# Three attentions of a decoder kernel rebuilt: fp32 scores of four heads in one burst of eight

## What is computed

```python
q = (query @ Wq.T + bq) * SCALING          # query = layernorm(x), key = value = ctx
k = key @ Wk.T + bk
v = value @ Wv.T + bv
scores = jnp.einsum('bhld,bhsd->bhls', q, k) + attn_mask[None, None, :, :]
scores = jnp.where(key_padding_mask[:, None, None, :], -jnp.inf, scores)
probs = jax.nn.softmax(scores.astype(jnp.float32), axis=-1)
attn = jnp.einsum('bhls,bshd->bhld', probs, v)
return attn.transpose(0, 2, 1, 3).reshape(query.shape[0], query.shape[1], E) @ Wo.T + bo
# x = x + jnp.tanh(g_xattn[2]) * that
```

## Time and profile before

| | |
|---|---|
| median of 3 executions | 862.42 us |
| lowest, highest | 861.39, 3578.52 us |
| the profiled execution: its own time | 862.37 us |
| its span | 860.4 us, 14382 instructions |
| its mean granted TensorE clock | 0.898 of 2.4 GHz |
| PE busy, and its weight loads | 702.3 us (82%), 396.0 us (46%) |
| DVE, ACT, POOL busy | 573.1 us (67%), 488.9 us (57%), 166.6 us (19%) |

### The profile page before, as it was taken

How to read it: one execution, slowest core, us unless ns; L and a number is a source line. 1 busy time by engine, 2 the same in 40 slices (tenths; PEclk the granted TensorE clock), 3 DMA queues, 4 the chain that set the end, 5 groups by cost and what they waited for, 6 DMA issues and landing times. The chain is left out here.

```text
span 860.4 us, 14382 instructions
## 1 busy us (share of the span) xinstructions
PE 702.3 (82%) x4728; PEld 396.0 (46%) x4728; DVE 573.1 (67%) x1765; ACT 488.9 (57%) x1323; POOL 166.6 (19%) x135
## 2 busy tenths in 40 slices
PE   4589994559997878999744899949999999869978
PEld 2266663336665323333222667635336666644322
DVE  3699995869996358667865999855316666436553
ACT  2288881259883568598812988812666556413201
POOL 8622000420000045536655000020000000000000
PEclk8689997769999768998885999979999999969999
DMA  8895004060000000000009200000000000000000
GB/s 310 169 319 177 2 7 69 23 126 2 2 2 2 0 1 0 1 0 1 1 0 180 41 2 2 2 26 0 1 0 1 1 2 2 1 1 1 0 1 24
DMA packets 22056, 32.26 MB, mean 38 GB/s; under 512 B 1760, under 2 KB 15712, under 8 KB 21216
## 3 DMA queue, kind: packets, MB, share of 16 engines
q1 hardware_dynamic: 21984, 31.36, 14.4%
HBM read 21.39 MB, written 9.96 MB: 36 GB/s over the span
## 5 line engine op out<-in xcount | busy, mean ns | idle before, releaser
L816 ACT ACTIVATE RING<-RING,NMX 128x256 f32<-128x256 f32 x384 | 190.7, 500 | 56.2 <-DVE NMX L1637 55.8
L1637 DVE CUSTOM_DVE_ANT_0 RING<-bank,ADJM 128x256 f32<-128x256 f32 x384 | 143.4, 413 | 23.5 <-DMA scratch<-RING 22.5
L1158 PE MATMUL bank<-W,RING 128*128 128x128 f32 x768 | 120.5, 282 | 15.6 <-ACT RING L828 13.9
L541 POOL TENSOR_TENSOR small<-small 128x8 f32<-128x8 f32 (+2 forms) x13 | 17.7, 1365 | 463.1 <-DVE small L1528 463.1
L1158 PEld LDWEIGHTS bank<-W,RING 128*128 128x128 f32 x768 | 91.7, 145 | 27.9 <-ACT RING L816 23.2
L1138 PE MATMUL bank<-ARENA 128*128 128x256 bf16 x384 | 77.8, 290 | 30.7 <-DMA ARENA<-scratch 25.7
L1649 DVE COPY RING<-bank 128x512 f32<-128x512 f32 x144 | 98.6, 686 | 1.2 <-PE bank L1158 0.8
L816 ACT ACTIVATION_READ_ACCUMULATOR RING<-RING,NMX 128x1 f32 x384 | 72.8, 190 | 0.0
L997 PE MATMUL bank<-XT,W 128*128 128x512 f32 (+2 forms) x118 | 62.2, 668 | 6.6 <-ACT XT L712 5.3
L728 ACT ACTIVATE RING<-bank,NMX 128x512 f32<-128x512 f32 x64 | 43.4, 683 | 41.8 <-PE bank L1062 21.2
L1280 PE MATMUL bank<-ARENA,W 64*128 64x512 f32 x180 | 62.3, 710 | 3.6 <-DVE ARENA L1830 2.3
(11 more groups left out here) (253 smaller groups left out, 1307.3 us busy)
## 6 DMA issues: line engine op xcount, KB each, us to landing
scratch<-ARENA SPq DMA_DIRECT2D x18, 256.0 KB, 3.2
ARENA<-scratch SPq DMA_DIRECT2D x6, 768.0 KB, 10.6
W<-in_weights SPq DMA_DIRECT2D x1, 2564.0 KB, 21.2
scratch<-RING SPq DMA_DIRECT2D x36, 64.0 KB, 3.0
ARENA<-scratch SPq DMA_DIRECT2D x12, 192.0 KB, 3.8
scratch<-RING SPq DMA_DIRECT2D x18, 128.0 KB, 2.9
ARENA<-scratch SPq DMA_DIRECT2D x6, 384.0 KB, 6.6
W<-in_weights SPq DMA_DIRECT2D x2, 1024.0 KB, 13.7
```

The lines of the kernel that those rows point to most:

```text
L816: nc.scalar.activation(P_OF(n)[:, q * S:(q + 1) * S], S_OF(n)[:, q, :], ACT.Exp, bias=NMX[:, 2 * t + q:2 * t + q + 1], scale=-1.0, accum_o ...
L1158: mm = nc.tensor.transpose(bk[:, o:o + P], P_OF(n)[:, i:i + P], ident)
L1637: nc.vector.tensor_tensor_reduce(out=S_OF(n)[:, q, :], in0=SBANK(n)[:, q * S:(q + 1) * S], in1=ADJM[:, b, q, :], scale=-1.0, scalar=BIG, o ...
```

## The change

- Scores are fp32 on the 8 rows of a head. Keys and queries are made with each head at the start of a 32-partition strip (`heads`: four narrow matmuls, 32 columns of the array each, into one bank), so that four heads lie in the four strips. The bf16 parts, the DRAM scratch and its DMAs, and the clearing of QS and KS go.
- A unit becomes one query tile of two heads. Every four units PE issues the eight score matmuls of four heads and two query tiles in one run, heads j = 0 to 3 into banks 0 to 3, and `Scores.fill` makes it wait for all eight DVE reductions of the run before. There is no second set of score banks.
- V has a column of ones behind each head's 8 columns (`PITCH` = 9), so that P times V gives the row sums too: the exponential loses `accum_out`. The result is transposed back (`ONE_T`), DVE takes a reciprocal and multiplies 64 elements, and once a sequence the packed result is transposed again (`BACK_T`) and multiplied by compact output weights WOC (one matmul and one row in place of four and one for each tile).
- DVE and ACT each copy every second unit's transposes.
- For attentions 0 and 2 only the keys of sequences 0 and 1 and the queries of sequence 0 are made ahead of the loop. Values, keys of sequences 2 and 3, and the queries of 1 and of 2 and 3 are made inside it (`extra`, at t = 4, 16, 8 and 24), in the score banks, between two runs of scores. Attention 1 has its keys and values made beside layer 0's linear layer, and only the two later pieces of queries are extras.
- In attention 0 only sequence 0's masks are made ahead of the loop; the rest (`other_masks`) is done by DVE at t = 6, POOL adding to it; POOL makes half of the later attentions' masks earlier.

The diff, cut to its core:

```diff
-LAG, PV_T, OTR_T, SEL_T, OUT_T = 3, 8, 9, 13, 27
-PT_SLOTS = 7
+LAG, PV_T, OTR_T, ONE_T, BACK_T, OUT_T, END_T = 3, 8, 9, 13, 27, 31, 16
...
+EXTRAS = [[("q", 0), ("v", 0), ("q", 1), ("k", 2), ("q", 2)], [("q", 0), ("q", 1), ("q", 2)],
+          [("q", 0), ("v", 0), ("q", 1), ("k", 2), ("q", 2)]]
...
# PE
+            def heads(out, name, g, rhs):
+                for j in range(HG):
+                    f = DH * (HG * g + j)
+                    mm = nc.tensor.matmul(out[PAD * j:PAD * j + PAD, :], w(name, f, f + PAD), rhs, start=True,
+                                          stop=True)
+                return mm
...
+            def extra(a, kind, k, scores):
+                x, (t0, t1) = extra_no(a, kind, k), PIECES[k]
+                scores.fill(pe, [(s_xa, 2 * x + 2), (s_xd, 2 * x + 2)])
+                for g in range(NG):
+                    if kind == "q":
+                        mm = heads(bank[g][:, 0:t1 - t0], f"wq{a}", g, XT[:, t0:t1])
...
-                        for q in range(2):
-                            mm = nc.tensor.matmul(bk[:, q * S:(q + 1) * S],
-                                                  QS[:, h, b * S + q * P:b * S + (q + 1) * P],
-                                                  KS[:, h // 2, b * S:(b + 1) * S], start=True, stop=True)
-                        mm.then_inc(s_s, 1)
+                        scores.fill(pe, [(s_max, 2 * base + 4 * m + 8)])
+                        for q in range(TPB):
+                            for j in range(HG):
+                                r = slice(PAD * j, PAD * j + DH)
+                                mm = nc.tensor.matmul(bank[j][:, q * S:(q + 1) * S],
+                                                      QT[r, g, b * S + q * P:b * S + (q + 1) * P],
+                                                      KT[r, g, b * S:(b + 1) * S], start=True, stop=True)
+                                if j % 2 == 1:
+                                    mm.then_inc(s_s, 1)
...
+                    if t >= ONE_T and (t - ONE_T) % 4 == 0 and (t - ONE_T) // 4 < UNITS // 4:
+                        for q in range(TPB):
+                            mm = nc.tensor.transpose(bank[7][:, q * P:(q + 1) * P],
+                                                     OTR[:, GG % 2, q * P:(q + 1) * P], ident)
+                        mm.then_inc(s_one, 1)
...
# ACT
                             nc.scalar.activation(P_OF(n)[:, i * S:(i + 1) * S], S_OF(n)[:, i, :], ACT.Exp,
-                                                 accum_out=SUMS[:, 2 * t + q:2 * t + q + 1]
...
# DVE
+                        if a != 1 and t == 4:
+                            dve.wait_ge(s_zero, 1 if a < 2 else 2)
+                            extra(a, "v", 0)
+                        if a == 0 and t == 6:
+                            other_masks()
+                        if a != 1 and t == 16:
+                            extra(a, "k", 2)
+                        if t in (8, 24):
+                            extra(a, "q", t // 16 + 1)
-                        dve.wait_ge(s_s, n + 1)
+                        dve.wait_ge(s_s, base + t // 4 * 4 + 3 + jj)
...
-                    if 0 <= u < UNITS and u % 4 != 2:
+                    if 0 <= u < UNITS and u % 2 == 0:
...
+                        dve.wait_ge(s_one, GG + 1)
+                        link(nc.vector.reciprocal(RS, src[:, :, :, DH:PITCH]))
+                        nc.vector.tensor_tensor(
+                            ON[:, i % 2, :, PAD * g:PAD * g + PAD].rearrange("p q (j d) -> p q j d", j=HG),
+                            src[:, :, :, 0:DH], RS.to_broadcast([P, TPB, HG, DH]), ALU.mult).then_inc(s_on, 1)
```

More of the change, by code:

```diff
@@ L515, in _ @@
-            read_keys(2)
-            queries(2)
+            compact(2)
             sp.wait_ge(s_var, 9)
@@ L545, in roots, with masks @@
                 root(TPB, NT)
-            def masks(a):
+            def masks(a, b0, b1):
                 if a > 0:
                     pool.wait_ge(s_max, 2 * UNITS * a)
-                for b in range(B):
+                for b in range(b0, b1):
                     for q in range(TPB):
@@ L1013, in turn, with biases @@
                     n_xn[0] += 1
-            def keys(a):
-                for c in range(NC):
-                    product(rk, [(w(f"wk{a}"), CT[:, half(c)])], s_fk)
+            def biases():
+                at = COL["cols"][0] + CI["bk0"][0]
+                for h in range(H16):
+                    g, j = h // HG, h % HG
+                    mm = nc.tensor.matmul(bank[5][PAD * j:PAD * j + PAD, 6 * g:6 * g + 6],
+                                          w("ident", DH * h, DH * h + PAD), W[:, at:at + 6], start=True, stop=True)
+                mm.then_inc(s_bk, 1)
@@ new lines, in heads, with keys, value_tiles @@
+            def heads(out, name, g, rhs):
[4 more added lines that the diff above has]
+                return mm
+            def keys(a, c):
+                for g in range(NG):
+                    heads(rh.fill(pe)[:, :], f"wk{a}", g, CT[:, half(c)]).then_inc(s_hf, 1)
+            def value_tiles(a, out, t0, t1):
+                for t in range(t0, t1):
+                    mm = nc.tensor.matmul(out[:, (t - t0) * D:(t - t0 + 1) * D], CT[:, t * P:(t + 1) * P],
+                                          w(f"wv{a}"), start=True, stop=True)
+                return mm
@@ new lines, in attention @@
+                            pe.wait_ge(s_to, 2 * GG + 2)
+                            pe.wait_ge(s_otr, GG)
+                            if G == 0:
+                                pe.wait_ge(s_ea, ra.n)
+                                if a != 1:
+                                    extra_done(a, "v", 0)
+                        for j in range(HG):
+                            f = PITCH * (HG * g + j)
+                            mm = nc.tensor.matmul(bank[6][PAD * j:PAD * j + PAD, 0:S], V[:, 2 * b + part, f:f + PAD],
+                                                  PT[:, GG % 2, j, part, :], start=(part == 0), stop=(part == 1))
```

578 lines of the change are left out of this document (279 added, 299 removed).

## The result

| | before | changed |
|---|---|---|
| median | 862.59 us (4 executions; the 862.42 ahead is of three) | 882.84 us (4 executions, 874.03 to 884.88) |
| ratio to before | 1 | 1.022, 95% interval 1.0133 to 1.0306 |
| profiled execution, its span | 862.37, 860.4 us | 882.24, 880.1 us |
| mean granted TensorE clock | 0.898 | 0.917 |

The kernel became slower by 20 us; whether by more than 2% the interval leaves open. The forecast was 856.5, with 880 as the upper end of its range. The page's first part, for the changed kernel: busy us, share of the span, instructions.

A forecast was written before the change was run, and what follows sets the result against it. Three engines near full bound the loop, with DMA latency at the starts. Starts -55.5, loops +53.6 and ends -4 sum to -5.9 from 862.37: 856.5 us, range 829 to 880.

The forecast's parts named there:

- Starts: Up to each attention's first reduction: -22.8, -11.5 and -21.2 us, together -55.5.
- The circle: Loop: scores wait for the previous group's last reduction, which waits for PE; 5.65 us a group against 4.95.
- Burst not serial: Loop: the run of eight score matmuls overlaps and takes about 1.0 us; serial would be 3.5 (rival, chance 0.07, 976 us).
- changes of shape cheap: Loop: a change of array shape costs PE 0.1 us, six in a group, without a whole drain of 0.17 each.
- Extras: Keys, queries and values made between bursts, uncovered: 14.3 us each in attentions 0 and 2, 7.2 in attention 1.
- The output row: Loop: 0.5 us added, listed beside the other masks at t = 6.
- The clock: Rival, chance 0.08: clock falls in the loop, +146 us at worst over 48 groups; one attention of it gives 905 us.
- a fall behind the other masks: Loop: PE idles during the masks made at t = 6, so the clock falls for some groups, 3.0 us.
- the rival as written: Loop at half clock, chance 0.08: the chain of 3.2 us grows by 3; one attention of it gives 905 us.
- Ends: Last reduction to the next statistics: about 9.2 us against 10.5 before, -4 for three.

The follow-up runs named there:

- e1: Changed kernel with transposes back, reciprocal and product two units later, behind a group's fourth unit: 867.33 us, ratio 1.0081.
- e5: Changed kernel with the burst of eight score matmuls issued twice in a row: 939.20 us, ratio 1.0918.
- e2: Changed kernel with one useless fp32 matmul of 512 columns before most bursts from the fourth on: 871.96 us, ratio 1.0141.
- e14: Changed kernel with useless matmuls before bursts in the loop and also at the three attentions' starts: 871.03 us, ratio 1.0114.
- e9: Against a kernel with extras in PE's gap and transposes back later (855.86 us): output matmuls into bank 6, addition to X two units later: 868.43 us.
- e12: Against a kernel with extras in PE's gap and transposes back later (855.86 us): useless matmuls at the starts alone: 844.67 us, ratio 0.9807.
- e8: Changed kernel with values, later keys and queries made in 512-column pieces in the gap before bursts: 860.90 us, ratio 0.9926.
- e13: e12 with one useless fp32 matmul of 256 columns before each burst that has no piece of the extras: 847.26 us, ratio 0.9848.

## Why the prediction was wrong

- **Starts** (-55.5): right, -54.6 by the rows. Attention 0's first reduction is at 21.0, where the forecast put it.
- **The circle**: right in mechanism; e1 and e5 moved it as they had to. Its size is a failed term: 5.65 in the sum, 5.88 measured. By the forecast's own steps: the burst to the transposes 1.08 for 1.0; transposes and P times V 0.59, 0.57, 0.58, 0.57 for 0.53 and 0.57, so the transposes back start at 3.39 for 3.2; back to reciprocal 0.48 for 0.55, reciprocal and product 0.39 for 0.4; the last reduction to the burst 0.58 for 0.48. Over the 36 groups, the last ones of each attention at 5.8, that is 7.3 us. The 0.1 in the last step goes with a second wait in PE's stream (e2), which the rows of before couldn't show.
- **Burst not serial, and changes of shape cheap**: right. The Trainium skill, TensorEngine Tiling (Array Packing), Key Properties, has a drain of TensorE at each change of tiling mode. The trace does not show a whole one: the burst is busy for 1.15 us, and the next shape starts at 1.08.
- **Extras** (14.3 and 7.2): right for the queries, whose 4.5 were 4.6. The values' 2.6 were 4.2 in attention 2 (from PE's first row to the burst), for the clock was half there (16 rows took 3.62 us, 463.11 to 467.34 with the emptying of the banks), and in e14, without a fall, still 3.2 (attention 2's first group took 7.47 us, attention 1's, which has no values, 4.32). The output row costs 1.1 us with the queries beside it (8.55 for 7.44 there); the sum had 0.5 for attention 0 and nothing for attention 2.
- **The clock** (a chance of 0.08): a failed term, and the one that the forecast had argued away. The sum had a fall behind the other masks (3.0) and at attention 1's start (2.4), and full clock elsewhere. What argued against more was that before's loops ran at 0.96 with transposes for half of PE's time; but there PE is busy 78.9 of 84.9 us, here 83.8 of 99.3 in attention 1, with a gap before every burst. The gap was in the forecast (PE waiting by about 1.2) and was not carried over to the clock. e2 fills the gap, and the falls from the fourth group on go; with e14 the clock's share is 14.7 us by the loops of the two profiles (325.7 to 311.0 from first to last reductions), and 12 by the times, as e14's starts and ends are some 3 us longer. Of the 14.7, 5.4 stood in the sum, so some 9 of the 26 missed are clock. Nearly all of it is attention 2's loop, where the sum had nothing and e14 took 10. It was also not the rival as written, a loop at half clock throughout, but single short stretches, of 1.5 us each. Why attention 2's loop had the most of them isn't shown: attention 1's has the same circle, PE busy for the same 84% of it, and stood at 0.95. The Trainium skill, TensorE: Matmul & The Clock Gate, Part 4, says that transposes do not count as PE-busy for the clock. These runs don't settle it: e14's loops are at 1.00 with transposes for about half of PE's time, but its filler is no transpose, and no run took the transposes away.
- **Ends** (-4 for three, +4.9 measured): a failed term, 8.9 us, as large as the clock's. The forecast gave 9.2 us from the last reduction to the statistics without laying it out; measured are 11.9, 11.9 and 12.7. Attention 1's after, where that reduction starts at 276.02:

```profile
277.33 0.63 PE L1183 MATMUL bank<-W,RING 128*128 128x128 f32 x4 [0.41 <-ACT ARENA L801]
...
281.18 1.07 PE L1202 MATMUL bank<-ARENA 128*32 128x256 f32 x16 [0.69 <-ACT ARENA L801]
...
287.23 0.61 DVE L1578 SCALAR_TENSOR_TENSOR X<-bank,small,X 128x128 f32<-128x128 f32 x2 [3.05 <-PE bank L1238]
```

  And before, where it starts at 265.86:

```profile
266.20 0.66 PE L1158 MATMUL bank<-W,RING 128*128 128x128 f32 x4
...
269.28 1.07 PE L1173 MATMUL bank<-RING,ARENA 128*32 128x256 f32 x16 [0.83 <-DVE RING L1649]
...
275.69 0.61 DVE L1544 SCALAR_TENSOR_TENSOR X<-bank,small,X 128x128 f32<-128x128 f32 x2 [3.23 <-PE bank L1204]
```

  The new tail, from the last P times V to the addition, is shorter, as thought: 6.05 us for 6.41. But that last P times V starts 5.16 us behind the last reduction, before 3.42: PE is 1.3 us from its next transposes when the reductions end (before 0.3), and has three transposes, two parts of P times V and a step back still to do one after the other. A loop that runs in bursts leaves more undone at its end. No run tried this apart, but the ones that move steps further back have longer ends still (e1: 13.4 to 14.6 us, e9: 15.1 to 17.4). Attention 2's 12.7 has all its output matmuls at half clock (0.77 to 0.80 us for 0.48), attention 1's 11.9 one pair of them.
- **The mixture of layer 1** is 3.4 us shorter, unforecast, and its cause wasn't tried.

So the step that failed is the loop's sum in its sizes, its clock and its end, and not the circle as such. By the profiles the account closes: of the 25.7 us, the loops are 19.3, of which 9.3 are clock and 10 stay with e14's fillers (the circle's size 7.3, the rest values, output row and masks, less a little in the first groups); the ends are 8.9 and the starts 0.9, with the mixture's 3.4 the other way.

## What to carry over

With one set of score banks, everything that DVE takes from PE between two bursts stands on one circle: put such a step behind the last reader of the banks, where it falls into the burst's shadow, and look for it again after each shift of a constant (e1's output step). Work that must be made inside such a loop belongs in the engine's gap before the burst and in a bank that nobody reads then. When a change gives PE a gap in every round, price the clock too, and test it with useless matmuls in the gap. And lay out what is still undone when the loop's last reduction ends: here that was 8.9 us of the 25.7 missed.

## What was not expected of the hardware

- Useless matmuls made kernels faster: 882.8 to 872.0 (e2), 855.9 to 844.7 (e12), and not the kernel before (862.75).
- From DVE's last reduction to the burst, 0.10 us more pass where PE's stream has another wait directly ahead of the one that ends last (0.58, 0.48), whether PE idles before it or not.
- The clock, and with it the time, can differ from execution to execution of one kernel: e8's ten spread over 19 us, with mean clocks of 0.901 (866.6 us) to 0.923 (847.4); e13's five over 2.4, at 0.935 to 0.939.
